# The last batch of a four-layer LoRA kernel in halves of 128 columns, and layer 3's second matrix placed by transfers

## What is computed

```python
x = x + _L0_cond_ref(x, itok_B_0_2, ...)              # x @ W.T + (x @ A[label]) @ Bw.T * 0.5
x = x + _L1_cond_ref(x, thresholds, deltas, zeropoints) # 8 quantisers, one picked for each value
x = x + _L2_cond_ref(x, weight, itok_B_3_7)           # einsum('bsi,boi->bso', x, w[adapter])
x = x + _L3_cond_ref(x, A, B, itok_B_3_7)             # (x @ B[adapter].T) @ A[adapter].T, rank 16
return x
```

## Time and profile before

| | |
|---|---|
| median of 3 runs | 455.46 us (455.26 to 455.71) |
| the profiled execution's own time | 455.72 us |
| its span (first to last instruction) | 453.9 us |
| PE busy | 445.7 us (98%) |
| DVE busy | 422.6 us (93%) |
| ACT busy | 363.6 us (80%) |
| chain that ended last | PE 75%, DVE 16%, issue 6% |
| mean granted clock | 0.997 of 2.4 GHz |

### The profile page before, as it was taken

How to read it: one execution, slowest core, us unless ns; L and a number is a source line. 1 busy time by engine, 2 the same in 40 slices (tenths; PEclk the granted TensorE clock), 3 DMA queues, 4 the chain that set the end, 5 groups by cost and what they waited for, 6 DMA issues and landing times.

```text
span 453.9 us, 7903 instructions
## 1 busy us (share of the span) xinstructions
PE 445.7 (98%) x3110; PEld 408.0 (90%) x3110; DVE 422.6 (93%) x402; ACT 363.6 (80%) x345; POOL 51.3 (11%) x61
## 2 busy tenths in 40 slices
PE   8999999999999999999999999999999999999985
PEld 7899999889998999889998999999898989998874
DVE  4699999999999998999899998999969999999993
ACT  5699999998699768977799775997578949698840
POOL 2300010002201010000101000111100201113000
PEclk9999999999999999999999999999999999999998
DMA  7973463496368835786459835496363645679222
GB/s 253 324 293 104 84 170 88 127 236 205 82 198 219 251 88 152 196 223 219 82 184 229 242 99 152 141 221 174 72 205 108 158 120 131 182 214 329 41 92 92
DMA packets 36649, 76.94 MB, mean 169 GB/s; under 512 B 4100, under 2 KB 14724, under 8 KB 35844
## 3 DMA queue, kind: packets, MB, share of 16 engines
q1 hardware_dynamic: 30708, 61.50, 40.9%
q0 software_dynamic: 5904, 14.94, 18.6%
HBM read 53.10 MB, written 8.39 MB: 135 GB/s over the span
## 4 chain that ended last, share of the span: by engine, by line
PE 75%; DVE 16%; issue 6%; ACT 1%; DVEq 0%; POOL 0%; POOLq 0%; ACTq 0%
PE l_ps L1026 35%; PE l_ps L1133 23%; PE l_ps L1145 6%; DVE quant L889 6%; DVE cand L863 4%; DVE cand L871 2%; PE l_ps L1034 2%; PE l_ps L1182 2%; PE bx_ps L1082 2%; PE bx_ps L1201 2%; PE l_ps L1068 1%; DVE x L841 1%; DVE x L940 1%; PE l_ps L1245 1%; DVE quant L883 1%
## 5 line engine op out<-in xcount | busy, mean ns | idle before, releaser
L1133 PE MATMUL l_ps<-x,w_sb 128*128 128x256 f32 x672 | 150.2, 380 | 0.0
L889 DVE COPY_PREDICATED quant<-mask,cand 128x2048 f32<-128x2048 int8 (+2 forms) x77 | 146.2, 1898 | 0.3
L1133 PEld LDWEIGHTS l_ps<-x,w_sb 128*128 128x128 f32 x672 | 125.9, 190 | 18.3 <-issue 2.1
L660 ACT ACTIVATE cand<-x,inv_delta 128x2048 f32<-128x2048 f32 (+2 forms) x88 | 134.3, 1527 | 5.3 <-DVE quant L883 3.7
L670 ACT ACTIVATE mask<-magnitude,thr_bias 128x2048 fp8e5<-128x2048 f32 (+2 forms) x77 | 117.4, 1524 | 5.6 <-DVE quant L889 5.4
L863 DVE TENSOR_SCALAR cand<-cand,delta 128x2048 f32<-128x2048 f32 (+2 forms) x88 | 87.5, 994 | 7.4 <-ACT cand L660 7.2
L871 DVE TENSOR_SCALAR cand<-cand,lower,upper 128x2048 f32<-128x2048 f32 (+2 forms) x88 | 92.7, 1053 | 0.4
L1026 PE MATMUL l_ps<-x_hi,w_hi 128*128 128x256 f32 x496 | 82.8, 289 | 0.0
L1026 PE MATMUL l_ps<-x_hi,w_lo 128*128 128x256 f32 x496 | 79.7, 283 | 0.0
L1026 PE MATMUL l_ps<-x_lo,w_hi 128*128 128x256 f32 x496 | 79.6, 283 | 0.0
L1026 PEld LDWEIGHTS l_ps<-x_hi,w_hi 128*128 128x128 f32 x496 | 68.7, 191 | 5.0 <-issue 3.7
(11 more groups left out here) (110 smaller groups left out, 420.8 us busy)
## 6 DMA issues: line engine op xcount, KB each, us to landing
w_sb<-w SPq DMA_DIRECT2D x60, 384.0 KB, 3.8
out<-x SPq DMA_DIRECT2D x32, 256.0 KB, 2.3
x_raw<-x SPq DMA_DIRECT2D x14, 512.0 KB, 6.1
w_edge<-w SPq DMA_DIRECT2D x28, 256.0 KB, 3.8
w_lo<-w_edge POOLq DMA_DIRECT2D x28, 256.0 KB, 4.9
x_lo<-x_raw POOLq DMA_DIRECT2D x6, 1024.0 KB, 8.5
x<-a SPq DMA_DIRECT2D x7, 512.0 KB, 3.5
cand<-w SPq DMA_DIRECT2D x4, 512.0 KB, 8.2
```

What stands on the lines that cost most here:

```text
L660: act.activation(cand[:, c % CANDS, 0:n], x2_unit(u), ACT.Identity, bias=ROUND, scale=inv_delta[:, k:k + 1]).then_inc(rounded, 1)
L889: dve.copy_predicated(y, mask[:, m % MASKS, 0:n].bitcast(I8), t).then_inc(merged, 1)
L1133: last = nc.tensor.matmul(l2_bank(b, q)[:, i * S:(i + 1) * S], w2_block(b, o, k), x2[:, b % SLOTS, k * S:(k + 1) * S], start=(i == 0 and k ...
```

## The change

It has two parts. First, the last batch's layer 2 runs in products of 128 columns: `last_product` issues each weight block twice, once for each half t of the tokens (HS = 128), in the first and second part; the third part, the rank product, its split, layer 3, the add and the stores run half by half, with half 0 ahead of half 1. Each half has one bank of l0_ps for outputs 0 to 3 (g = 0) and one for 4 to 7 (g = 1); DVE finishes g = 0, and g = 1 is added up on PE with one multiply of 512 columns and copied out by ACT. Second, a3 is loaded once, as 128x128 (64 KB); ACT and DVE split it there, SP writes high, low, high to a buffer in memory (`put_a3`), and POOL brings that to the two groups of 48 partitions (`spread_a3`). The unused partitions of a3_split are zeroed once, by POOL, at the start. `split_a3` moves to step 1 of the unit for batches 0 to 5 and to the end of the last batch's second unit for batch 7.

```diff
             def load_a3(b, adapter):
...
+                if b > 0:
+                    sp.wait_ge(a3_lo_done, b)
+                sp.dma_start(a3_raw[:, :], a3[bass.ds(adapter, 1)].rearrange("l p w -> p (l w)"))\
                   .then_inc(a3_loaded, 16)
+
+            def put_a3(b):
+
+                sp.wait_ge(a3_lo_done, b + 1)
+                for i, half in enumerate((a3_hi, a3_lo, a3_hi)):
+                    sp.dma_start(a3_mem[i * R3:(i + 1) * R3].rearrange("r (c w) -> (r c) w", c=T),
+                                 half[:, :].bitcast(F32)).then_inc(a3_put, 16)
...
                 for o in range(RING, T):
                     load_w2(s - 1, o, last_adapter)
+                    if o == T - 3 and s < B - 1:
+                        put_a3(s - 1)
...
+            pool.memset(x2[:, 0, 0:D], 0.0).then_inc(a3_zeroed, 1)
...
+            pool.tensor_copy(a3_split[:, :], x2[:, 0, 0:D]).then_inc(a3_zeroed, 1)
...
+            def spread_a3(b):
+
+                pool.wait_ge(a3_put, 3 * 16 * (b + 1))
+                if b > 0:
+                    pool.wait_ge(l3_done, 4 * b)
+                for side in range(2):
+                    first = side * P // 2
+                    pool.dma_start(a3_split[first:first + 3 * R3, :], a3_mem).then_inc(a3_spread, 16)
...
             def split_a3(b):
                 dve.wait_ge(a3_hi_done, b + 1)
-                dve.scalar_tensor_tensor(a3_split[:, :], a3_split[:, :].bitcast(F32), not_a3_hi, a3_raw(b),
-                                         ALU.mult, ALU.add).then_inc(a3_split_done, 1)
+                dve.tensor_tensor(a3_lo[:, :], a3_raw[:, :], a3_hi[:, :].bitcast(F32), ALU.subtract)\
+                    .then_inc(a3_lo_done, 1)
...
+            def last_product(o, w, v, start=False):
+                for t in range(2):
+                    nc.tensor.matmul(last_tile(last_bank, t, o), w, v[:, t * HS:(t + 1) * HS], start=start, stop=False)
...
+            def last_third_part(t, g):
+                b = B - 1
+                for o in range(g * HALF, (g + 1) * HALF):
+                    for k in range(PARTS[2], T):
+                        last = nc.tensor.matmul(last_tile(last_bank, t, o), w2_block(b, o, k),
+                                                x2[:, b % SLOTS, k * S + t * HS:k * S + (t + 1) * HS], start=False,
+                                                stop=(o % HALF == HALF - 1 and k == T - 1))
+                last.then_inc(last_l2_done, 1)
...
+            def last_add_up(t):
+
+                nc.tensor.matmul(last_bank(t, 1), ident[:, :], last_x3(t, 1), start=True, stop=False)
...
-            last_layer2(2)
-            for q in range(4):
-                low_rank3(B - 1, q)
-            for q in ADDED_UP:
-                add_up(q)
-            for q in LAST_ORDER:
-                layer3(B - 1, q)
+            pe.wait_ge(x2_done, LAST + 3)
+            last_third_part(0, 0)
+            last_third_part(0, 1)
+            last_third_part(1, 0)
+            last_low_rank3(0, 0)
+            last_low_rank3(0, 1)
+            last_third_part(1, 1)
+            last_low_rank3(1, 0)
+            last_add_up(0)
+            last_low_rank3(1, 1)
+            pe.wait_ge(a3_spread, 2 * 16 * B)
+            pe.wait_ge(last_bx_split_done, 1)
+            for g in range(2):
+                last_layer3(0, g)
+            last_add_up(1)
+            pe.wait_ge(last_bx_split_done, 2)
+            for g in range(2):
+                last_layer3(1, g)
```

More of the change, by code:

```diff
@@ L21 @@
 HALF = T // 2
+HS = S // 2
 QUAD = 32
@@ L512, in _ @@
                 add_edges(s - 1, 3)
+                spread_a3(s - 1)
                 if s < SPLIT:
@@ L520, in _ @@
                 add_last_edge(o)
+            spread_a3(B - 1)
         @block.scalar
@@ L700, in between @@
                 elif s < B - 1:
[L701 to L702 removed]
+                    if j == 1:
+                        split_a3(s - 1)
+                        if s + 2 < B:
+                            split_batch(s + 2)
                     if j == 3:
[L704 removed]
                         if low_batch(s):
@@ L1170, in last_first_part, with last_second_part @@
                         for k in range(EDGE):
-                            nc.tensor.matmul(l2_bank(b, o // 2)[:, o % 2 * S:(o % 2 + 1) * S],
-                                             w[:, k * P:(k + 1) * P], v[:, k * S:(k + 1) * S],
-                                             start=False, stop=False)
-            def last_layer2(part, quarters=range(4)):
+                            last_product(o, w[:, k * P:(k + 1) * P], v[:, k * S:(k + 1) * S])
+            def last_second_part(tiles):
@@ L1176, in last_layer2 @@
                 b = B - 1
-                pe.wait_ge(x2_done, LAST + part + 1)
-                for q in quarters:
-                    for i in range(2):
-                        o = 2 * q + i
-                        for k in range(PARTS[part], PARTS[part + 1]):
-                            last = nc.tensor.matmul(l2_bank(b, q)[:, i * S:(i + 1) * S],
-                                                    w2_block(b, o, k),
-                                                    x2[:, b % SLOTS, k * S:(k + 1) * S],
-                                                    start=False, stop=(i == 1 and k == T - 1))
-                    if part == len(PARTS) - 2:
-                        last.then_inc(l2_done, 2)
+                pe.wait_ge(x2_done, LAST + 2)
@@ new lines, in last_second_part @@
+                for o in tiles:
+                    for k in range(PARTS[1], PARTS[2]):
+                        last_product(o, w2_block(b, o, k), x2[:, b % SLOTS, k * S:(k + 1) * S])
+            def last_third_part(t, g):
[6 more added lines that the diff above has]
+                last.then_inc(last_l2_done, 1)
@@ new lines, in last_low_rank3 @@
+            def last_low_rank3(t, g):
+                b = B - 1
+                if t == 0 and g == 0:
+                    pe.wait_ge(b3_loaded, (b + 1) * 16)
+                    pe.wait_ge(low_split_done, B)
+                    pe.wait_ge(out_done, 4 * b)
+                pe.wait_ge(last_x3_done, 2 * t + g + 1)
+                w = P // 2
+                for k in range(g * HALF, (g + 1) * HALF):
+                    last = nc.tensor.matmul(last_bx(t)[k % 2 * w:(k % 2 + 1) * w, :], b3_tile(b, k, w),
+                                            last_tile(last_x3, t, k), start=(k < 2), stop=(k >= T - 2))
+                if g == 1:
+                    last.then_inc(last_bx_done, 1)
@@ new lines, in last_add_up, with last_layer3 @@
+            def last_add_up(t):
+                nc.tensor.matmul(last_bank(t, 1), ident[:, :], last_x3(t, 1), start=True, stop=False)
+            def last_layer3(t, g):
+                for o in range(g * HALF, (g + 1) * HALF):
+                    last = nc.tensor.matmul(last_tile(last_bank, t, o), a3_split[:, o * P:(o + 1) * P],
+                                            bx_split[:, t * HS:(t + 1) * HS], start=(g == 0),
+                                            stop=(g == 0 or o == T - 1))
+                last.then_inc(last_l3_done, 1)
```

194 lines of the change are left out of this document (99 added, 95 removed).

## The result

The changed kernel takes 461.73 us (median of 4 runs, 461.18 to 462.49) beside 455.58 us for the kernel before in the same comparison: ratio 1.0129, 95% interval 1.0113 to 1.0145. It is 1.3% slower. The forecast was 461.8 us. The profiled execution took 461.18 us, with a span of 459.4 us.

A forecast was written before the change was run, and what follows sets the result against it. DVE bounds the stretch from 332 to 438 us by 2.4 us, with PE next; PE bounds the rest. Third part at 442.75 + end 14.04 + 3.4 + 1.8 = 462.0, less 0.26: 461.8 us; range 453.5 to 466.0.

The forecast's parts named there:

- Prices of a PE record: Last batch on PE: a 128-column record, float32r or float32, costs 0.119 us, paced by its weight load.
- The stream-paced rival: 128-column records paced by their stream: float32r 0.0625 us, float32 0.108 us; time 453.7 us; chance 0.11.
- its neighbour: 128-column records at 0.08 us: PE's growth of 2.0 us just fills the gaps; 455.2 us, no change; chance 0.04.
- float32's pace: Narrow float32r products at 0.216 us: +15.0 us for the split products, time 472.6 us; chance 0.12.
- PE's growth: Ahead of the third part: first part +0.71, split products +5.71, second part +0.71, together +7.1 us on PE.
- PE's gaps: PE's four idle gaps between 332 and 438 us, 2.40 us in sum, can all close.
- The rival of SP's wait: SP's put of a3 delays weight tiles; if transfers land twice as late, 2 us a batch, 474 us; chance 0.03.
- The third part's start: Last batch's third part on PE starts at 438.02 + 7.13 - 2.40 = 442.75 us; quantising gives 442.2 to 443.3.
- ACT's stall: ACT waits for PE's late rank product until about 433.9 us, and again for the sum, until about 436.5.
- The end: From the third part's start to ACT's last copy: 10.48 + 3.56 = 14.04 us, 1.6 more than before.
- The a3 part: Cheaper a3 splits put DVE 1.7 us earlier in its stretch from 332 to 438 us; added queue waits cost 0.
- The five splits before and all of ACT's are hidden: Cheaper a3 splits before batch 6's unit, and ACT's, save nothing; PE hides them, and ACT is busy 80%.

The follow-up runs named there:

- experiment 1: The kernel before with the change's a3 part alone, last batch still in 256-column records: 455.07 us, 0.9980 of before; run again 454.84 us, 0.9973.
- experiments 4 and 5: e3 and e10, in this order, both the changed kernel with one edit against the store wait: 460.72 us and 460.82 us.
- experiment 6: The changed kernel without its a3 part: a3 loaded as 128x1024 and split in place, last batch in halves; 461.52 us, 1.0127 of before.
- experiment 3: The changed kernel with the 96 split products of 128 columns cut into 192 of 64 on the same weights: 490.02 us, 1.0727 of before.
- e10: The changed kernel with POOL's last spread waiting until batch 6's four stores have landed: 460.82 us, 1.0102 of before.
- e3: The changed kernel with the last batch's x3 kept in the raw x buffer, so drains don't wait for batch 6's stores: 460.72 us, 1.0094 of before.
- e5: The kernel before with the a3 part alone, batch 6's put moved behind the weight ring's four loads on SP: 455.07 us, 0.9985 of before.
- e11: The changed kernel with last x3 in the raw x buffer, batch 6's put behind the ring's loads, its spread behind POOL's last adds: 461.42 us, 1.0113.

## Why the prediction was right, point by point

- **Prices of a PE record.** The mechanism holds: the load of 128 columns is the pace, for both types. The size was 0.112 us and not 0.119. The 256-column float32r record, from which the price was taken, lies a little above what its load needs. The stream-paced rival asked for 0.0625 us, its neighbour for 0.08, float32's pace for 0.216: none occurred. By the Trainium skill (TensorE: Matmul & The Clock Gate, "Back-to-back issue gap") a sustained load and multiply pair at 128 columns would take about 81 ns; this case's trace, with 0.112 us, does not agree, and the measurement decides.
- **PE's growth.** 0.119 gave 7.13 us. The traces have 10.85 - 6.03 = 4.8 us for the split products and 0.8 for the two other parts together, waits left out (first part 7.00 to 7.47, second 7.47 to 7.77): 5.6 us. This term was 1.5 us too large.
- **PE's gaps.** Four gaps of 2.40 us were to close. The first three did; the one ahead of the third part stayed, at 0.50 us. The waits for w_sb, 0.17 and 0.45 us, are new. The prediction had put all waits on queues at 0: 0.6 us were missed there, 0.5 at the gap that stayed. The rival of SP's wait did not occur, though all 60 weight tiles landed later, in 4.9 us at the median instead of 3.8; only ahead of the last batch's first part did the cover run out.
- **The third part's start.** 438.02 + 5.6 - 2.40 + 0.50 + 0.62 = 442.3 us; the trace has 441.46. The rest was there before any of this: PE was 0.8 us ahead at 331.3 us already. 0.5 of it is the start of the program, which varies from execution to execution (the same kernel reaches this record at 332.46 us in experiment 1 and at 331.24 when run again). The other 0.3 is the change's own, and is told under the a3 part.
- **ACT's stall.** It occurred as told, though longer: ACT waited 5.60 us for PE's rank product, DVE 5.22 us behind it, and quantising caught up just in time, as PE's 0.50 us ahead of the third part show.
- **The end.** 14.04 us were forecast, 15.06 measured. The step that failed is "DVE's drains fit in between": it took DVE's inputs from PE alone and left out that the drains overwrite what batch 6's stores still read. The last spread, costed at nothing, doubles the time of these stores and makes the wait; the a3 split of 1.2 us on DVE, which would have covered part of it, is gone with the change. Without the wait the tail takes 14.29 us (experiments 4 and 5), still 0.25 more than forecast, although the record is cheaper. The rank products took 0.073 us a record and not 0.0625, 0.3 us in all, and half 0's add of 512 columns 1.06 us (451.38 to 452.44) and not 0.86.
- **The a3 part.** Forecast 1.7 us earlier on DVE: its add at 409.57 us stands at 408.05 in experiment 1. Counted from PE's record at 332 us (332.03 before, 332.46 there) it is 1.95 us earlier. But PE had to be able to follow. Alone the part brought 1.0 us, and 2 us in the kernel with tile 3 last. "The five splits before and all of ACT's are hidden" was wrong by 0.30 us: that the time before 332 us gets shorter was the prediction's own sign of a misread chain. At 324.8 us PE waited for ACT's copy of the rank product, in the trace of before:

```profile
324.77 0.30 PEld L1208 LDWEIGHTS bx_ps<-parts,bx_sum 128*128 128x128 f32 x2 [0.24 <-ACT parts L595]
```

  With the a3 part ACT is there in time. From the `close0` record ahead of this wait to the next one it is 3.72 us before (324.46 to 328.18), 3.73 in experiment 6, which has no a3 part, and 3.42 in all twelve traces with it.
- **The sum** for the profiled execution was 462.0 us, and it took 461.18. The third part's start came 1.3 us early (about 1.5 by the records and 0.8 by the earlier place, with waits of 1.1 the other way), the tail took 1.0 more, and from the last copy to the end of the span 2.9 us passed instead of 3.4. Then the median lies 0.55 us above this execution, where before it lay 0.26 below: another 0.8, which brings the forecast to 0.1 us from the median. The sign and the mechanism of the records were well founded; that closeness was luck, with errors of 0.8 to 1.5 us in several terms.

## What to carry to other kernels

Cutting a product's columns in two on the same weights nearly doubles its cost where the load is the pace: here a float32r record of 0.119 us became twice 0.112, while a float32 record of 0.216 became the same twice 0.112 and so cost almost nothing more. Ask for each transfer added what else starts in the same microsecond and who waits for it, and for each operation removed which transfer was landing meanwhile. When PE waits for the last tile of a ring, try the order in which it takes the tiles; moving things on the queues did not help here.

## What the runs showed of the hardware

- A multiply of 64 columns on 128-column weights costs 0.111 us at the full clock, as one of 128 does (experiment 3); on 64-column weights one of 128 columns costs 0.073 us (the changed kernel).
- Such a row can cost the clock: during the 64-column records the granted clock went from 1.00 to 0.50 with PE busy throughout, and the kernel took 28 us more than the changed one, where the added records alone would have cost 10.7. The 128-column records of the changed kernel ran for 10.85 us at 1.00.
- Transfers of 384 KB in all, beside 1 MB of stores, took the stores from 2.2 us (e10, e6 and the kernel before) to 4.8 (the changed kernel and e3).
- With some 400 GB/s moving when it is issued, the same 384 KB weight tile lands in 3.3 us in one kernel (e5) and 5.6 in another (e11), with PE's wait for it from 0 to 1.67 us. What decides it within that range was not settled.
